# Gated MLP: rows split in row layout and turned by DMA transposes, three pairs of up banks, two up tiles ahead

## The reference, cut to what matters

```python
h = shift_token(x)                 # second half of the features comes from the row before
mu = h.mean(-1, keepdims=True)
var = h.var(-1, keepdims=True)
h = (h - mu) / jnp.sqrt(var + 1e-05) * lg + lb
h = h @ w1 + b1                    # 256 -> 2 * 682
a, g = jnp.split(h, 2, axis=-1)
h = a * jax.nn.gelu(g, approximate=False)
x = x + h @ w2 + b2                # 682 -> 256
```

## Time and profile before

| | us |
|---|---|
| median of 3 runs | 4296.58 |
| lowest, highest | 4293.78, 4302.39 |
| profiled execution, its own time | 4296.06 |
| its span, first to last instruction | 4294.4 |

### The profile page before, as it was taken

One profiled execution on the slowest core, in us unless ns is written; L12 is line 12 of the kernel. 1 busy time (PEld: TensorE's weight loads), 2 busy tenths in 40 slices (PEclk: granted clock), 3 DMA queues, 4 the chain that ended last, 5 costly groups with the idle time before them and its releaser, 6 DMA issues. The chain is left out here.

```text
span 4294.4 us, 94790 instructions
## 1 busy us (share of the span) xinstructions
PE 3835.2 (89%) x38292; PEld 2167.2 (50%) x38292; DVE 3330.0 (78%) x5467; ACT 2558.9 (60%) x3449; POOL 1191.1 (28%) x966
## 2 busy tenths in 40 slices
PE   7999999769998969998986999999999999866996
PEld 4788888535655535555553332332333333334664
DVE  5688988779985569985687889999998978584444
ACT  3566666646553435653443777787888887744553
POOL 1022321267761067771141000000000000033552
PEclk9999999889999989999997999999999999977998
DMA  1010100133330033430072000000000000034664
GB/s 63 5 40 28 43 25 25 41 70 64 63 51 28 0 63 66 65 55 9 0 160 47 9 9 2 9 2 2 9 2 2 9 2 9 4 100 93 117 134 111
DMA packets 325878, 175.39 MB, mean 41 GB/s; under 512 B 239508, under 2 KB 316520, under 8 KB 324968
## 3 DMA queue, kind: packets, MB, share of 16 engines
q1 hardware_dynamic: 302856, 133.88, 14.8%
q0 software_dynamic: 13440, 21.24, 2.9%
q10 hardware_dynamic: 9184, 14.68, 1.4%
HBM read 77.81 MB, written 38.58 MB: 27 GB/s over the span
## 5 line engine op out<-in xcount | busy, mean ns | idle before, releaser
L2257 DVE TENSOR_REDUCE s_tops<-ps 128x2 f32<-128x1024 f32 (+3 forms) x1152 | 1252.2, 1132 | 143.2 <-PE ps L2143 103.6
L2226 ACT ACTIVATE s_weights<-ps 128x1024 f32<-128x1024 f32 (+3 forms) x1152 | 1092.5, 952 | 344.3 <-PE ps L2156 193.8
L2178 PE MATMUL ps<-s_weights,v_flat 128*32 128x256 f32 (+1 forms) x8704 | 692.1, 390 | 7.4 <-ACT s_o_t L2232 6.1
L2137 PE MATMUL ps<-keys,s_q 48*128 48x512 f16 (+3 forms) x2304 | 435.0, 375 | 46.0 <-DVE s_tops L2257 26.0
L2156 PE MATMUL ps<-s_q,keys 50*128 50x512 f16 (+3 forms) x2304 | 434.0, 374 | 46.9 <-DVE s_tops L2257 33.3
L2293 POOL CAST s_shift<-s_minus_top 128x16 f16<-128x16 f32 x32 | 6.3, 196 | 1429.9 <-DVE s_minus_top L2264 1429.9
L583 PE MATMUL ps<-a_qt,a_kt 128*128 128x256 f16 x3072 | 375.3, 273 | 3.8 <-POOL s_ones L538 3.8
L2156 PEld LDWEIGHTS ps<-s_q,keys 50*128 50x128 f16 x2304 | 112.2, 93 | 512.3 <-issue 246.7
L1174 PE MATMUL ps<-attention_w,la_yt 128*128 128x512 f16 x1152 | 289.3, 399 | 37.8 <-DMA la_yt<-la_y_parts 30.3
L583 PEld LDWEIGHTS ps<-a_qt,a_kt 128*128 128x128 f16 x3072 | 300.9, 98 | 40.3 <-POOL s_ones L538 4.2
L1249 ACT ACTIVATE la_weights<-ps 128x1024 f32<-128x1024 f32 x124 | 126.8, 1023 | 291.5 <-PE ps L1164 291.5
(11 more groups left out here) (372 smaller groups left out, 7158.0 us busy)
## 6 DMA issues: line engine op xcount, KB each, us to landing
ex_whole<-in_L_ffn_w_dram ACTq DMA_DIRECT2D x14, 1024.0 KB, 10.2
qk_parts<-a_parts SPq DMA_DIRECT2D x64, 128.0 KB, 4.3
keys<-qk_parts SPq DMA_DIRECT2D x48, 128.0 KB, 5.7
s_q<-qk_parts SPq DMA_DIRECT2D x48, 128.0 KB, 5.0
x<-in_x_dram SPq DMA_DIRECT2D x8, 512.0 KB, 9.3
attention_w<-attention_split SPq DMA_DIRECT2D x2, 2048.0 KB, 9.1
la_table<-in_rotary_dram SPq DMA_DIRECT2D x64, 64.0 KB, 2.1
a_table<-in_rope_dram POOLq DMA_DIRECT2D x8, 512.0 KB, 6.1
```

The source lines that it names most:

```text
L2137: mm = pe.matmul(m.ps[:, bank, 0:width], b.q[rows(half, KEY_PARTS * L1_DH), place % 2, pair, t * P:(t + 1) * P], m.keys[rows(half, KEY_PAR ...
L2178: mm = pe.matmul(m.ps[h * QUAD:(h + 1) * QUAD, OUT, begin:end], m.v_flat[:, first:first + QUAD], weights[:, a % 2, h, begin:end], start=(k ...
L2226: act.activation(weights[:, a % 2, 2 * pair:2 * pair + 2, skip:CHUNK], m.ps[:, bank:end + 1, skip:CHUNK], ACT.Exp).then_inc(s["exp"], 1)
L2257: dve.tensor_reduce(tops[:, u % 2, :, i % 2, t, c], m.ps[:, bank:end + 1, 0:width], AX.X, ALU.max).then_inc(s["max"], 1)
```

## The change

- The rows are split before they are turned. Gain and offset are applied to `normed` in row layout, by two POOL instructions for each chunk (`gain`), with gain and offset spread over all partitions by two new loads (`lng_row`, `lnb_row`). For chunk 0 DVE does both. ACT rounds the whole chunk to its high part in one instruction (`high`), at the first gelu of the chunk before. DVE subtracts in one instruction (`parts_low`), after the second product of that chunk.
- SP turns both parts with four DMA transposes for each chunk (`turn`), straight into `ht`. PE's transposes, ACT's two evictions with their copies, and DVE's two subtractions are gone. The shift by one row is now a read one column to the left (`EDGE - k`), and POOL copies the last column of a chunk in front of the next (`edge`).
- PSUM banks 0 and 1 come free and become a third pair: tile e waits for tile e-3 (`RING`). Two up tiles of the next chunk go ahead of the down product (`AHEAD`).

```diff
-    TURN_AT = ET - 4
-    NORMED_BY = {1: 0, 2: 1, 4: 2, 5: 3}
+    RING, AHEAD = 3, 2
+    EDGE = 16
+    HIGH_AT, LOW_AT = 0, 1
+    NORMED_BY = {2: 0, 3: 1, 4: 2, 5: 3}
...
+                for to, name in ((lng_row, "ln_g"), (lnb_row, "ln_b")):
+                    sp.dma_start(to[:, :], layer_of(a[name], layer).rearrange("o d -> (o d)").partition_broadcast(P)).then_inc(s["rows_in"], 16)
...
+                def turn(c):
+                    sp.wait_ge(s["low"], c + 1)
+                    if c:
+                        need(sp, s["ht"], 16 * TPC * c)
+                        need(sp, s["a_mm"], ET * (c - 1))
+                    for j in range(TPC):
+                        at = EDGE + j * P
+                        sp.dma_start_transpose(ht[:, c % 2, :, :, at:at + P].rearrange("p a k t -> p (a k) t"),
+                                               parts[:, c % 2, j, :, :].rearrange("p a d -> p (a d)")).then_inc(s["ht"], 16)
+
+                turn(0)
                 move_down(sp, m, s, 1)
                 if not last:
                     load_attention(sp, m, a, layer + 1, s["next_in"])
                 move_up(sp, m, s, 1)
+                for c in range(1, CHUNKS):
+                    turn(c)
...
+                def edge(c, u):
+                    need(pool, s["ht"], 16 * TPC * (c + 1))
+                    need(pool, s["a_mm"], ET * c)
+                    pool.tensor_copy(ht[:, 1 - u, :, 1, EDGE - 1:EDGE], ht[:, u, :, 1, EDGE + CHUNK - 1:EDGE + CHUNK]).then_inc(s["edge"], 1)
+
+                def gain(c, u):
+                    need(pool, s["normed"], c + 1)
+                    whole = normed[:, u, :, :]
+                    pool.tensor_tensor(whole, whole, lng_row[:, :].unsqueeze(1).broadcast_to([P, TPC, D]), ALU.mult).then_inc(s["gained"], 1)
+                    pool.wait_ge(s["gained"], c)
+                    pool.tensor_tensor(whole, whole, lnb_row[:, :].unsqueeze(1).broadcast_to([P, TPC, D]), ALU.add).then_inc(s["whole"], 1)
...
-                def ht_low(c, u):
-                    need(dve, s["a_mm"], ET * (c - 1))
-                    for k in range(KD):
-                        need(dve, s["ht_high"], KD * c + k + 1)
-                        dve.tensor_tensor(ht[:, u, 1, k, :], ht_whole[:, u, k, 0:CHUNK], ht[:, u, 0, k, :], ALU.subtract).then_inc(s["ht"], 1)
+                def parts_low(c, u):
+                    dve.wait_ge(s["high"], c + 1)
+                    dve.scalar_tensor_tensor(parts[:, u, :, 1, :], normed[:, u, :, :], 1.0, parts[:, u, :, 0, :], ALU.mult, ALU.subtract).then_inc(s["low"], 1)
...
                 norm(0, 0)
+                need(dve, s["normed"], 1)
+                dve.wait_ge(s["rows_in"], 32)
+                whole = normed[:, 0, :, :]
+                dve.tensor_tensor(whole, whole, lng_row[:, :].unsqueeze(1).broadcast_to([P, TPC, D]), ALU.mult).then_inc(s["first_gained"], 1)
+                dve.wait_ge(s["first_gained"], 1)
+                dve.tensor_tensor(whole, whole, lnb_row[:, :].unsqueeze(1).broadcast_to([P, TPC, D]), ALU.add).then_inc(s["first_whole"], 1)
+                norm(1, 1)
+                parts_low(0, 0)
...
                 half_rows_on_vector(dve, m, s, 1)
-                norm(1, 1)
-                ht_low(0, 0)
                 rows_on_vector(dve, m, s, 1)
...
+                def high(c, u):
...
+                    act.copy(parts[:, u, :, 0, :], normed[:, u, :, :]).then_inc(s["high"], 1)
...
                 def up(c, u, tiles):
-                    need(pe, s["ht"], KD * (c + 1))
+                    need(pe, s["ht"], 16 * TPC * (c + 1))
...
                 def step(c, u):
-                    up(c, u, range(1, TURN_AT + 1))
+                    up(c, u, range(AHEAD, ET))
                     if exists(c + 1):
-                        turn(c + 1, 1 - u)
-                    up(c, u, range(TURN_AT + 1, ET))
-                    if exists(c + 1):
-                        up(c + 1, 1 - u, range(1))
+                        up(c + 1, 1 - u, range(AHEAD))
                     down(c, u)
```

More of the change, by code:

```diff
@@ L1442, in gated_mlp @@
         after = statistics_buffers(nc, ctx, "gm") if last else None
-        with stage(nc, f"gm{layer}", "weighted", "x", "consts", *(f"x_{n}" for n in STATISTICS), "next_in", "w2_in", "minus", "first", *ROW_STATISTICS, "zeroed", "before", "normed", "turned", "ht_whole", "ht_high", "ht", "a_mm", "g_mm", "gelu",
+        with stage(nc, f"gm{layer}", "weighted", "x", "consts", *(f"x_{n}" for n in STATISTICS), "next_in", "w2_in", "minus", "first", *ROW_STATISTICS, "zeroed", "before", "edge_high", "edge_low", "edge", "normed", "rows_in", "first_gained", "first_whole", "gained", "whole", "high", "low", "ht", "a_mm", "g_mm", "gelu",
                    "hid_whole", "hid_high", "hid", "out", "b2", "y") as (block, s):
@@ L1475, in _ @@
             def _(pool):
-                credit(pool, s["b2"])
+                credit(pool, s["b2"], s["edge"])
                 pool.memset(hid[:, :, :, ET - 1, :], 0.0).then_inc(s["zeroed"], 1)
@@ L1482, in bias, with step @@
                     pool.tensor_tensor(y, y, b.b2[:, :].unsqueeze(1).broadcast_to([P, TPC, D]), ALU.add).then_inc(s["b2"], 1)
+                def edge(c, u):
[8 more added lines that the diff above has]
+                    pool.tensor_tensor(whole, whole, lnb_row[:, :].unsqueeze(1).broadcast_to([P, TPC, D]), ALU.add).then_inc(s["whole"], 1)
+                def step(c, u):
+                    bias(c, u)
+                    if exists(c + 1):
+                        edge(c, u)
+                    if exists(c + 2):
+                        gain(c + 2, u)
+                pool.wait_ge(s["rows_in"], 32)
+                gain(1, 1)
                 rows_on_gpsimd(pool, m, s, 1)
-                in_pairs(pool, CHUNKS, bias)
+                for c in range(CHUNKS):
+                    step(c, c % 2)
                 if last:
@@ L1491, in _ @@
             def _(dve):
-                credit(dve, s["normed"], s["ht"], s["hid_whole"], s["hid"], s["y"])
+                credit(dve, s["normed"], s["hid_whole"], s["hid"], s["y"])
                 def norm(c, u, rows=range(TPC)):
-                    need(dve, s["turned"], KD * (c - 1))
+                    if not isinstance(c, int) or c >= 2:
+                        dve.wait_ge(s["low"], c - 1)
                     for j in rows:
@@ L1645, in gelus @@
                         rows = slice(0, sizes[e])
-                        act.activation(gelu[rows, e % 2, :], m.ps[gate_rows(e), 3 + 2 * (e % 2), :], ACT.Gelu, bias=b.b1[gate_rows(e), 1, e:e + 1],
+                        act.activation(gelu[rows, e % 2, :], m.ps[gate_rows(e), 2 * (e % RING) + 1, :], ACT.Gelu, bias=b.b1[gate_rows(e), 1, e:e + 1],
                                        scale=1 / SCALE).then_inc(s["gelu"], 1)
                         if e:
-                            high(e - 1)
-                        if e == TURN_AT and exists(c + 1):
-                            scaled(c + 1, 1 - u)
-                    high(ET - 1)
-                scaled(0, 0)
+                            hid_high(e - 1)
+                        if e == HIGH_AT and exists(c + 1):
+                            high(c + 1, 1 - u)
+                    hid_high(ET - 1)
+                high(0, 0)
                 act.wait_ge(s["zeroed"], 1)
@@ L1683, in up @@
                 def up(c, u, tiles):
-                    need(pe, s["ht"], KD * (c + 1))
+                    need(pe, s["ht"], 16 * TPC * (c + 1))
+                    if isinstance(c, int) and c == 0:
+                        pe.wait_ge(s["edge_low"], 1)
+                    else:
+                        need(pe, s["edge"], c)
                     for e in tiles:
```

64 lines of the change are left out of this document (27 added, 37 removed).

## The result

The changed kernel takes 4323.89 us (median of 4 runs, 4321.15 to 4325.59) against 4296.72 of the kernel before on the same chip: a ratio of 1.0063, with a 95% interval of 1.005 to 1.0075. Slower, as forecast, but by 27.2 us instead of 14, and above the range. A second series gave 4321.81 us, a ratio of 1.0055 (1.0039 to 1.0072). The profiled execution took 4323.46 us, its span 4321.5.

What follows compares the result with a forecast made beforehand. PE was taken to bound the stage. Layer 0 at +5.5 us, layer 1 at +5.8 and the clock at +3 made +14 from the profiled 4296.06: 4310 us, range 4292 to 4322.

Steps and rivals of the forecast that it cites:

- T(1): Start of PE's first up matmul behind a down product, beginning chunk 1; forecast 12.0 and 11.1 us late.
- The new wait: Before the tiles ahead in every middle chunk, PE waits 1.2 us for rows; four transposes take 6.3.
- rival B: The four transposes land before PE asks, so faster or not slower: 4292 or 4285 us; chance 0.13.
- The saving of a middle chunk: Each middle chunk gets shorter by 0.74 us in layer 0 and by 0.54 in layer 1.
- one whole POOL instruction, 2.7: Upper bound in us, per chunk of layer 1, for POOL's work holding up DVE; 0.2 was taken.
- The start: At each stage's start `move_down` and DVE's first product come 10.4 us later, chunk 1 12.0 and 11.1 later.
- 3 for the clock: PE's wait in chunk 0 may lower its granted clock: 0 to 3 us a layer, 1.5 taken.
- The end: The last chunk keeps its wait and slow down product, but one more tile is already done: -2.6 us.
- C: Bursts land in 7.2 us, POOL holds DVE, or clock falls in short waits: 4323 to 4328 us; chance 0.15.
- A: The forecast itself: late rows in every chunk and a late start, 4310 us, own range 4303 to 4318; chance 0.64.
- D: The late start is hidden before DVE's first product, taking off up to 2 x 10.4 us: 4289; chance 0.08.
- Third pair and other edits at nothing: ACT's changed work, the third bank pair, POOL's gain and `edge` were all counted at no time.

Runs made afterwards that it cites:

- earlier split: Changed kernel with ACT's rounding and DVE's subtraction for chunk c+2 moved into chunk c, for chunk 1 before the first product: 4299.34 us, ratio 0.9995.
- the later bias: Changed kernel with POOL's last bias in layer 1 held until three low parts of chunk 7's `hid` are made: 4315.82 us.
- the old order: Changed kernel with only the stage start put back: half sums right behind the first norm, `move_down` issued before the first four transposes: 4320.40 us, ratio 1.0051.
- both edits: Changed kernel with the earlier split and the old order at the stage start together: 4294.81 us, ratio 0.9989.
- PE's transposes for chunk 0: Earlier split kernel with chunk 0 turned by PE, DVE doing chunk 1's gain and offset, and the next weights' load later: 4279.49 us; again 4277.76.
- the run with two tiles ahead: Kernel before with only two up tiles of the next chunk ahead of the down product instead of one, two bank pairs kept: 4282.53 us, ratio 0.9971.

## Why the prediction was wrong, step by step

The forecast is 13 us short: 6.9 of them lie between T(1) and T(7) of the two stages, 5.7 outside the stages.

- **The new wait**: right in kind and nearly in size. The burst takes 6.4 to 7.0 us, mostly 6.6, for the 6.3 that I took; rival B's early landing did not come. PE waited 1.05 to 1.77 us in the middle chunks against 1.2 and 1.4.
- **The saving of a middle chunk, 0.74 and 0.54 us**: the step that failed. T(1) to T(7) was to fall by 3.9 and 2.7 us; it fell by 1.4 in layer 0 and rose by 1.6 in layer 1. Three causes. First, small terms in layer 0: where no loop head stands before the chunk, PE resumes at T + 10.6 instead of T + 10.4 (the burst is 0.3 longer, its first issue 0.1 sooner behind the product), and the chunk takes 23.2 for 23.0; in chunk 1 the burst took 7.0, another 0.4. That a chunk without a wait takes 21.92 and not 21.8 (earlier split) costs nothing here, since the wait covers it. Second, DVE's first product was put at T + 0.71 in every chunk, and I had read it in chunk 1, which does not follow a loop head; behind one it is at T + 1.25 and 1.21, 0.5 us more in chunks 2 and 4 of layer 0. In layer 1 it is at T + 0.95 in chunks 2 and 4, 0.3 more each; the other chunks there take the 23.2 of the forecast. Third, chunk 6 of layer 1 took 26.96 where the sum has 23.2, 3.8 us: "one whole POOL instruction, 2.7" was the upper bound of the cost of a chunk in layer 1, but two of them close together made the wait 2.1 longer than the 1.2 of the others, and the lower clock behind it cost 1.7. The run with the later bias shows the cause.
- **The start**: the numbers, 12.0 and 11.1 and 3 for the clock, 26.1, agree with the measured +14.4 and +11.7, 26.1. That the sum fits so closely is luck: with 1.5 for the clock in each layer, layer 0 has 0.9 more than forecast and layer 1 0.9 less. The reason was half right. I let `move_down` and the first product carry the whole delay; with the old order T(1) came only 3.4 us earlier in layer 0 and 1.0 in layer 1. PE's start behind chunk 0's rows, +16 us against +8.4, is as long a chain. I had written that PE itself starts at 1319.2 and took no bound from it. The runs with both edits and with PE's transposes for chunk 0 show it. The first-chunk clock dip came in layer 0 alone, behind waits of 3.65 and 3.82 us (24 matmuls in 6.69 and 7.05, +1.3 and +1.7); in layer 1 the waits were 2.45 and 2.12, under the 3.0 to 3.7 forecast, and the matmuls took 5.36.
- **The end**: -2.6 twice, measured -3.4 and -1.9, within what two profiles of one kernel differ. The last down product, behind a wait of 2.97 to 2.99 us, took anything from 7.6 to 10.5 us in the profiles of this series.
- **Outside the stage**: the prediction had nothing there and gave no reason for it; the two pairs of profiles show +5.7. Without it the time would have been some 4318 (an estimate, 4323.9 less 5.7), inside the range. Against mere variation speaks that the means of five and eleven profiles differ by 7.5; against an effect of the new stage, that a third of this stands in a stage that runs before it. What makes it, no run here shows.
- **The rivals**: the time fell into C's, 4323 to 4328, but not by C's mechanisms: bursts took 6.6 and not 7.2, and DVE's first piece was held ahead of each of chunks 2 to 5 of layer 1, but by 1.1 to 1.3 us and at little cost; only ahead of chunk 6 were both held. So the sum is A's, with chunk 6 and the other stages on top. D is out: the late start was not hidden.
- **Third pair and other edits at nothing**: right for this kernel, as two pairs cost nothing. With the rows in time it could be worth the 0.6 us behind a loop head that the run with two tiles ahead waits; that is an estimate, no run compares the two.

Of the two pages cited: by the Trainium skill, page DMA: Bandwidth & Descriptors, section Issuing engines are not separate DMA queues, the time to initiate a DMA is usually small beside the DMA itself; here it is 1.27 us of SP for a transfer that lands 2.5 after its issue, and halving the number of issues took 1.7 of 6.6 us away. By the Trainium skill, page SBUF — State Buffer, section SBUF: two separate sides, a DVE instruction with two inputs in SBUF and a POOL instruction that reads SBUF exclude one another on a shared port pair for a whole instruction; the 1.21 us pieces, which have two such inputs and take 2.3 to 3.2 beside POOL's instructions of 2.35, agree.

## What to carry to other kernels

Work that leaves the bounding engine must come back to it in time: ask first at which instruction the producer of the moved work stands, and put it a whole chunk earlier before anything is counted as saved. Count the issues of a DMA burst before its bytes, and give the first chunk, which nothing precedes, its own way in. When a stall at a stage's start has a known cause, look for a second chain of the same length before pricing its removal. And take a change with several parts apart: here the second tile ahead, a change of order alone, gave 9 us of MLP with none of the new waits.

## What was not expected of the hardware

- A small DMA right behind a 2 MB load on the same queue was issued over 7.01 us and landed 8.5 after its issue began, where 1.56 us of issue do in layer 1 without the load. This is not new with the change: the same issue took 3.39 us in layer 0 before and 3.58 in the changed kernel, and in all of these it ends 0.4 to 2.0 us behind the landing of the load.
- POOL's work beside DVE stretched DVE's instructions by some 2 us, nearly the 2.35 of a whole POOL instruction: 1.21 us became 3.18, and ahead of the first chunk a subtraction of one column took 2.30. Moving the last bias only changed which instruction was held (a low part of 0.68 then took 2.23).
- Behind a loop head DVE's first product comes some 0.5 us later in layer 0; no engine it waits for is named, only "issue". What takes the time there, no run separates.
